# A fused eight-layer transformer kernel: expert weights held until the first gathers have landed, float16 token tables, and GpSimd work cut up and moved

## The reference

```python
# L1_ffn: attention, then the two best experts of each token
x = x + o @ w_o + b_o
h = _layernorm(x, ln2_g, ln2_b).reshape(B * S, D)
topv, topi = jax.lax.top_k(h @ gate_w + gate_b, 2)       # weights: softmax of topv
# L2_ffn: every expert with a sigmoid above 0.5
weights = probs * (probs > 0.5)
# L3_ffn: the best expert of each token
mask = (max_ind == e)[:, None]
# in all three, for each expert e
y = act(h @ W1[e] + b1[e]) @ W2[e] + b2[e]               # relu, relu, gelu
x = x + weight[token, e] * y
```

## Time and profile before

| what | value |
|---|---|
| median of 3 runs | 2282.51 us (2282.28 to 2283.62) |
| the profiled execution's own time | 2278.04 us |
| its span, first to last instruction | 2276.3 us |
| TensorE busy | 1962.3 us (86%) |
| DVE / ACT / GpSimd busy | 1069.3 / 910.1 / 755.3 us |
| mean granted TensorE clock | 0.932 of full speed |
| self-attention: first matmul of scores to the end of the projection stage | 546.3 to 984.5 us |
| m1: start of the stage, first expert matmul | 984.8, 1026.5 us |
| m2: the same | 1375.2, 1417.4 us |
| m3: the same | 2075.9, 2110.7 us |

### The profile page before, as it was taken

One profiled execution on the slowest core, in us unless ns is written; L12 is line 12 of the kernel. 1 busy time (PEld: TensorE's weight loads), 2 busy tenths in 40 slices (PEclk: granted clock), 3 DMA queues, 4 the chain that ended last, 5 costly groups with the idle time before them and its releaser, 6 DMA issues. The chain is left out here.

```text
span 2276.3 us, 39023 instructions
## 1 busy us (share of the span) xinstructions
PE 1962.3 (86%) x12253; PEld 1425.4 (63%) x12254; DVE 1069.3 (47%) x2424; ACT 910.1 (40%) x1930; POOL 755.3 (33%) x790
## 2 busy tenths in 40 slices
PE   6699989744999999849999945999999998696898
PEld 5476656512233232338999844999999997364797
DVE  6875834635777777253332246222222222576221
ACT  2413642132777777613333321333333333264132
POOL 0134952405000000043444333334444343585243
PEclk9799999876999999969999976999999999798899
DMA  4004300123111111075222118422122221205611
GB/s 159 19 1 146 101 1 1 32 76 94 37 36 49 42 37 36 2 245 156 33 35 36 28 53 292 115 36 36 31 36 35 35 34 27 68 1 177 221 32 26
DMA packets 124399, 151.26 MB, mean 66 GB/s; under 512 B 27066, under 2 KB 104731, under 8 KB 124171
## 3 DMA queue, kind: packets, MB, share of 16 engines
q1 hardware_dynamic: 93533, 117.61, 15.9%
q0 software_dynamic: 24288, 31.81, 8.6%
q10 hardware_dynamic: 6480, 0.59, 0.3%
HBM read 114.35 MB, written 37.36 MB: 67 GB/s over the span
## 5 line engine op out<-in xcount | busy, mean ns | idle before, releaser
L1902 PE MATMUL banks<-m_rowsT,x_normT 128*128 128x128 f32 x4032 | 479.0, 278 | 11.9 <-issue 7.6
L1902 PEld LDWEIGHTS banks<-m_rowsT,x_normT 128*128 128x128 f32 x4032 | 468.5, 194 | 29.0 <-issue 11.5
L1911 PE MATMUL banks<-m_w,m_hT 128*128 x2016 | 461.3, 382 | 7.3 <-ACT m_hT L2145 5.6
L1911 PEld LDWEIGHTS banks<-m_w,m_hT 128*128 128x128 f32 x2016 | 375.6, 191 | 56.4 <-issue 8.4
L2155 ACT ACTIVATE m_y<-banks,m_weight 128x256 f32<-128x256 f32 x126 | 59.6, 473 | 636.7 <-PE banks L1914 526.6
L2585 ACT ACTIVATE sh_pT<-banks 128x1024 f32<-128x1024 f32 x256 | 250.7, 1024 | 26.1 <-PE banks L2544 26.0
L2145 ACT ACTIVATE m_hT<-banks,m_bias 128x128 f32<-128x128 f32 x848 | 229.7, 387 | 65.6 <-PE banks L1902 61.4
L1821 POOL DMA_INDIRECT scratch_acc<-m_y,m_row_ids x106 | 169.6, 1600 | 124.8 <-ACT m_y L2155 82.9
L2609 DVE TENSOR_REDUCE sh_mhalf<-banks 128x1 f32<-128x512 f32 x308 | 194.2, 683 | 35.5 <-PE banks L2493 35.5
L2079 DVE TENSOR_SCALAR x_normT<-m_w 128x2048 f32 x129 | 158.3, 1227 | 77.0 <-issue 69.8
L1807 POOL COPY m_row_ids<-m_ids 128x1 int32 x117 | 52.1, 445 | 337.0 <-DMA scratch_acc<-m_y,m_row_ids 215.2
(11 more groups left out here) (404 smaller groups left out, 2745.1 us busy)
## 6 DMA issues: line engine op xcount, KB each, us to landing
m_w<-L_W SPq DMA_DIRECT2D x32, 1024.0 KB, 13.4
m_w<-L1f_W SPq DMA_DIRECT2D x16, 1024.0 KB, 13.6
a_bt<-bias SPq DMA_DIRECT2D x16, 616.0 KB, 3.9
...
```

Source lines behind the costliest of these rows:

```text
L1902: mm = pe.matmul(ps[:, H_BANK[u] + f // 4, f % 4 * P:(f % 4 + 1) * P], w1_tile[:, u, k, f * P:(f + 1) * P], rowsT[:, u, k, :], start=(k == ...
L1911: mm = pe.matmul(ps[:, Y_BANK[u], 0:D], hT[:, u, f, :], w2_sb[:, bass.ds(e, 1), f, :], start=(f == 0), stop=(f == FB - 1 and not biased))
```

## The change

Six edits, all in the routed layers and what leads to them:

1. **SP's order in the routed layers.** The store of `x` is taken from behind the stored rows to behind the two transfers of expert 1, and ahead of it stands a wait for the second gather (`rows_in[1]`). So expert 1 is issued right behind the rows, and `x` and experts 2 to 7 only when the second gather has landed.
2. **Float16 tables.** The one-hot matrices are float16, in which a token number minus 2048 is exact. One product (`tokens_at`) stands for the two, the matmuls of the table have half as many columns, and one DVE instruction for two makes `ids`.
3. **The bias addition in the self-attention** is 16 instructions of 128 x 256, the t-th behind `m_split` t + 1.
4. **The projection stage**: GpSimd adds `x` tile by tile for 12 tiles without waiting for moments, with the reciprocals of groups 0, 1 and 2 behind tiles 6, 10 and 11.
5. **m1** begins on GpSimd with the addition of the last four tiles to `x` (128 x 1024), for which DVE waits before tile 12.
6. **Reciprocals of m2** are all made in the routed stage (`ready=0` for `ready=2`) and none in the plain cross-attention.

GpSimd also makes one more small constant in the first layer's stage (`firsts`, `tokens` for `back`).

```diff
@@ routed_layer, SP
                 if e == 0:
                     for g in range(NCH):
                         sp.wait_ge(tile_normed, 4 * g + 4)
                         sp.dma_start(table[g * CH:(g + 1) * CH, 0:D].rearrange("(t p) d -> p t d", p=P), xn[:, 4 * g:4 * g + 4]).then_inc(stored, 16)
+                if e == 1:
+                    sp.wait_ge(rows_in[1], 16)
                     sp.dma_start(stream.rearrange("(t p) d -> p t d", p=P), x[:]).then_inc(x_stored, 16)
@@ routed_layer, GpSimd
+            if joins_last:
+                pool.tensor_tensor(x[:, NT - 4:NT], x[:, NT - 4:NT], xn[:, NT - 4:NT], ALU.add).then_inc(joined, 1)
@@ routed_layer, TensorE
-                    at = ps[:, TABLE_BANK, g * 2 * W:(g + 1) * 2 * W] if local else ps[:, TABLE_BANK, 0:2 * W]
-                    mm = pe.matmul(at, lane_hits[:, g % 2, :, t], id_parts[:, g, :, :, t],
+                    at = ps[:, TABLE_BANK, g * W:(g + 1) * W] if local else ps[:, TABLE_BANK, 0:W]
+                    mm = pe.matmul(at, lane_hits[:, g % 2, :, t], tokens_at[:, g, :, t],
@@ routed_layer, DVE
             for t in range(NT):
+                if joins_last and t == NT - 4:
+                    dve.wait_ge(joined, 1)
...
-            link(dve.tensor_tensor(id_parts[:, :, 0], tile_hits, back_b[:].unsqueeze(1).unsqueeze(1).broadcast_to([P, G, W, NT]), ALU.mult))
-            dve.tensor_scalar(id_parts[:, :, 1], tile_hits, lane[:], None, ALU.mult).then_inc(parts_done, 1)
+            dve.tensor_tensor(tokens_at, tile_hits, tokens[:].unsqueeze(1).unsqueeze(1).broadcast_to([P, G, W, NT]), ALU.mult).then_inc(parts_done, 1)
...
-            link(dve.tensor_scalar(high_at, high, float(P), float(TOK), ALU.mult, ALU.add))
-            dve.tensor_tensor(ids_at, high_at, low, ALU.add).then_inc(ids_done, 1)
+            dve.tensor_scalar(ids[:, 0:COLS], ps[:, TABLE_BANK, 0:COLS], float(TOK), None, ALU.add).then_inc(ids_done, 1)
@@ self_attention, GpSimd
-                pool.tensor_tensor(acc[:], acc[:], w["bo"][:].unsqueeze(1).broadcast_to([P, NT, D]), ALU.add).then_inc(bias_added, 1)
+                for t in range(NT):
+                    pool.wait_ge(m_split, t + 1)
+                    pool.tensor_tensor(acc[:, t, :], acc[:, t, :], w["bo"][:], ALU.add).then_inc(bias_added, 1)
@@ token_projection, GpSimd
-            for g in range(NCH):
+            def reciprocals(g):
                 own = slice(4 * g, 4 * g + 4)
-                if g < NCH - 1:
...
+            for t in range(NT - 4):
+                pool.wait_ge(y_sb, t + 1)
+                pool.tensor_tensor(core.x[:, t, :], core.x[:, t, :], acc[:, t, :], ALU.add).then_inc(joined, 1)
+                if t in (6, 10):
+                    reciprocals(t // 4 - 1)
+            reciprocals(2)
@@ program
-            routed_layer(core, "m2", "threshold", ..., ready=2)
+            routed_layer(core, "m2", "threshold", ..., ready=0)
```

67 lines of the change are left out of this document (26 added, 41 removed).

## The result

| | before | changed |
|---|---|---|
| median, us | 2282.4 (2278.84 to 2283.62, 4 runs) | 2301.64 (2297.45 to 2302.27, 4 runs) |
| ratio | | 1.0083, 95% interval 1.0066 to 1.0100 |
| profiled execution, span | 2276.3 | 2299.9 |
| mean granted clock | 0.932 | 0.923 |

The account below looks back on a forecast made before the run. TensorE, busy 86% of the span, bounds the kernel; only its waits can change. Terms -9.0 - 5.4 + 0.4 + 14.9 + 12 + 2 = +14.9 us, added to the median: 2297.4; 8 in 10 range 2281 to 2309.

Parts of the forecast that it names:

- The signal behind the issues: Routed layers' start: `experts_ready` rises only after five SP issues, at T + 8.3, delaying first expert matmuls, +14.9 us in sum.
- T: Moment a routed layer's second gather lands and SP goes on: predicted 1019.8 in m1, 1413.2 in m2, 2103.3 in m3.
- Rival A: Routed layers' start: the queue takes `x` and two experts without holding SP; -18 us, median 2264; chance 0.12.
- Rival B: Fifth tile: late start but no stalls, additions land in some 6 us; median 2283 to 2289; chance 0.14.
- for the lower clock behind them: Lower TensorE clock behind the fifth-tile stalls in m1 and m2: 2 us added.
- Self-attention: Cut bias addition removes TensorE's wait on L2619: 7.8 us plus 1.2 for the clock, gain 9.0, bounds 7 to 10.
- a delay for tile 12: m1's start: GpSimd's 128 x 1024 addition and reciprocals make DVE's tile 12 about 0.5 us late.
- Rivals C and D: C: expert comes too late, 3 to 8 us in m3, chance 0.06; D: hold does not free gathers, +9 us, 0.06.
- m2's reciprocals: Moved reciprocals: 2.3 us gained in plain attention, m2's normalisation ends 2.7 later; sum +0.4 us, bounds -1.5 to +3.
- The range: Whole kernel: 2289 to 2308 us from the bounds of the forecast's parts; 8 in 10 range 2281 to 2309.

## Why the prediction was right

The forecast was 2297 us, the median is 2301.6: the sign and the mechanism were right, the size 4.6 us short. In spans the sum is 8.7 us short (14.9 for 23.6), and about half of that is the profile of before, which lies 4.4 us below its median.

*The signal behind the issues* was the heart of it, and it is what happened in all three layers. From the list to the first expert matmul it took 7.2, 8.2 and 4.5 us more than before, where the prediction has 7.6, 8.5 and 4.6. Two small errors cancel in this. DVE went on at T + 9.3, 8.9 and 9.2 us and not T + 8.3, and the first matmul came at T + 12.0, 11.5 and 11.4 and not 11.3, 11.0 and 11.0; but T itself was 5.4, 6.3 and 5.4 us behind the list and not 6.5, 7.3 and 6.0. (The rows give 1.54 + 2.52 us for the start of m1's second gather, where the prediction reads 1.05 + 2.52; with SP quiet it was 2.5.) Three runs bear it out: the signal alone made early gives 15.6 us back, the store of `x` taken out of its way gives 13.7. The evidence used, a load of `x` that delayed the next issue by 2.6 us, was the right one: the issue behind `x` took 2.52 us. The 5.6 us in the earlier trace rows are three issues and not four, which together with the one behind `x` are the four that stand in the way.

*Rival A* fell as argued, and the runs show how near it was. Without `x` in front, experts 2 and 3 pass in 3.4 us. That the queue blocked SP hung on the place of one line.

*Rival B* (late start, no stalls) fell: the first additions took 7.6, 9.1 and 8.9 us beside the weights, and TensorE waited 5.25, 6.42 and 6.60 us. Against before that is 5.3, 5.7 and 3.0, 14.0 in sum for the 12 predicted. The weights were on their way until some 43 us behind T, for 42 predicted; 14.7 MB at 366 GB/s are 40.

*The step that was mis-sized* is the 2 us "for the lower clock behind them". By the rows the clock cost 2.2 us at m1's fifth tile (L1908 5.79 and not 3.62) and 1.6 at m2's, and it also cost 1.3 us at m1's first tile (6.53 and not 5.22), since TensorE came to it out of a wait of 12.6 us. I had put the clock behind the stalls only, not behind the longer wait at the start. With m2's first tile (0.35) and m3's fifth (0.2) that is 5.7 and not 2.

*Self-attention.* The wait went as predicted. In this trace 6.9 came and not 9.0; the mean of the twelve profiles with the cut addition is 407.7, against 416.9 and 416.6 without, so 9.0. In the stretch itself the term was right, and this one profile had a lower clock. By the whole time the bias alone gave 6.4 us, with 9.0 just inside its interval. The Trainium skill's rule that was weighed there (page SBUF — State Buffer, section Who interferes with whom) didn't strike at L2630: the small addition ran from 559.92 to 560.65, and that instruction, L2623 now, came at 561.81 and took 0.28 us as before. In m1, where I took the addition only as a delay for tile 12, DVE's second normalising instruction stood still for 2.05 us. It has one tensor in SBUF and not two, so the form of the rule that was weighed does not name it; the same section says that a `tensor_scalar` can contend as well, in its two-port modes. The trace agrees with that, with 2454 ns against a median of 401, though no run here shows in which mode it ran. That was 2.0 us, of which I had 0.5 in the sum.

*Rivals C and D.* Behind the first copy of each layer there is one wait on `experts_ready` in the trace, 3.76 us of DVE at m1's second copy (1024.30), and it cost TensorE nothing: its next matmuls waited 1.00 us, for ACT. SP's release came 5.4 us behind the list in m1. Both rivals are out, and the hold did free the gathers. What the prediction did not ask is whether the freed time would be given back at the fifth tile in every form of the hold.

*m2's reciprocals.* From the reload in m1 to m2's list it took 88.7 us before and 86.9 changed: 1.9 less, for 1.4 predicted (0.4 - 1.8).

*The range.* "2289 to 2308 from the bounds of its parts" can't be worked out again: the bounds as written, added up on either side, give 2265 to 2311.
